# The distance stage of an attention kernel: key part first, by columns, query part second, by rows, stored 16 rows at a time

## What is computed

```python
dist_idx = pos_l - pos_r + M - 1
pos_emb = dist_emb[dist_idx]
rel_q = jnp.einsum('bhld,lrd->bhlr', q, pos_emb)
rel_k = jnp.einsum('bhrd,lrd->bhlr', k, pos_emb)
scores = (scores + rel_q + rel_k) / jnp.sqrt(jnp.asarray(D, scores.dtype))
```

## Time before, and how the profile is read

| | |
|---|---|
| median of 3 runs | 3550.53 us (3544.78 to 3551.01) |
| the profiled execution | 3545.81 us, span 3544.3 us |
| distance stage, first add to next stage's first DMA | 401.23 to 1520.00 us |
| first add of the first tile to first add of the last tile | 1077.2 us for 31 tiles |
| mean granted clock of PE in that stretch | 0.66 of full speed |

### The profile page before, as it was taken

How to read it: one execution, slowest core, us unless ns; L and a number is a source line. 1 busy time by engine, 2 the same in 40 slices (tenths; PEclk the granted TensorE clock), 3 DMA queues, 4 the chain that set the end, 5 groups by cost and what they waited for, 6 DMA issues and landing times. The chain is left out here.

```text
span 3544.3 us, 68683 instructions
## 1 busy us (share of the span) xinstructions
PE 2759.8 (78%) x18124; PEld 1931.5 (54%) x18124; DVE 2474.6 (70%) x6213; ACT 1770.8 (50%) x3509; POOL 703.2 (20%) x715
## 2 busy tenths in 40 slices
PE   4676588787787787748888877888888588888887
PEld 2343577777677777625555544555555344444443
DVE  5665477676777677648888877888888566666664
ACT  2343354444454444348888877888888411111111
POOL 2432000000000000012212211212221223333334
PEclk7888566666666666668999998999999789999999
DMA  3999799989989989799999999999999501111110
GB/s 112 221 224 213 162 311 348 294 337 291 331 302 333 299 333 321 309 261 271 268 272 278 267 257 268 268 272 274 270 272 275 180 32 63 62 62 62 62 62 20
DMA packets 905515, 807.89 MB, mean 228 GB/s; under 512 B 236808, under 2 KB 809536, under 8 KB 870832
## 3 DMA queue, kind: packets, MB, share of 16 engines
q1 hardware_dynamic: 840112, 640.95, 60.5%
q0 software_dynamic: 29440, 98.07, 13.0%
q10 hardware_dynamic: 35840, 67.12, 8.3%
HBM read 465.93 MB, written 340.05 MB: 227 GB/s over the span
## 5 line engine op out<-in xcount | busy, mean ns | idle before, releaser
L1059 ACT ACTIVATE t_e<-t_neg,t_low 128x512 f32<-128x512 f32 x1024 | 739.6, 736 | 232.2 <-DVE t_low L1001 228.9
L676 ACT ACTIVATE d_r<-d_pq 128x1024 f32<-128x1024 f32 x512 | 531.7, 1050 | 608.0 <-PE d_pq L633 604.6
L710 DVE TENSOR_TENSOR d_r<-d_pk,d_r 128x1024 f32<-128x1024 f32 x512 | 616.1, 1223 | 272.9 <-ACT d_r L676 134.0
L1001 DVE CUSTOM_DVE_ANT_0 t_neg<-t_ps,t_r 128x512 f32<-128x512 f32 x1024 | 671.3, 687 | 24.3 <-issue 24.3
L644 PE MATMUL d_pk<-d_win,d_k 96*128 96x128 bf16 x4096 | 513.8, 295 | 216.0 <-DVE d_r L710 181.0
L927 PE MATMUL t_pt<-t_ident,t_e 128*128 128x128 f32 x4096 | 639.4, 279 | 1.4 <-DVE t_eT L1009 0.9
L917 PE MATMUL t_ps<-t_kb,t_qa 96*128 (+1 forms) x1024 | 402.0, 393 | 251.6 <-DVE t_low L1001 202.2
L644 PEld LDWEIGHTS d_pk<-d_win,d_k 96*128 96x128 bf16 x4096 | 445.6, 183 | 248.5 <-DVE d_r L710 213.6
L927 PEld LDWEIGHTS t_pt<-t_ident,t_e 128*128 128x128 f32 x4096 | 513.7, 144 | 110.4 <-ACT t_eT L1066 16.7
L633 PE MATMUL d_pq<-d_win,d_q 96*128 96x128 bf16 x4096 | 498.2, 287 | 62.9 <-DVE d_q L693 45.2
L633 PEld LDWEIGHTS d_pq<-d_win,d_q 96*128 96x128 bf16 x4096 | 442.4, 187 | 80.2 <-DVE d_q L693 45.8
(11 more groups left out here) (134 smaller groups left out, 2509.1 us busy)
## 6 DMA issues: line engine op xcount, KB each, us to landing
r_scratch<-d_r SPq DMA_DIRECT2D x256, 1024.0 KB, 14.2
t_r<-r_scratch SPq DMA_DIRECT2D x1024, 256.0 KB, 5.3
d_q<-q_chunks_scratch ACTq DMA_DIRECT2D x64, 512.0 KB, 10.8
d_q<-q_chunks_scratch ACTq DMA_DIRECT2D x128, 256.0 KB, 14.1
t_kb<-k_chunks_scratch POOLq DMA_DIRECT2D x32, 512.0 KB, 19.9
q_chunks_scratch<-a_part SPq DMA_DIRECT2D x96, 128.0 KB, 3.6
q_rows_scratch<-a_part SPq DMA_DIRECT2D x96, 128.0 KB, 2.2
k_chunks_scratch<-a_part SPq DMA_DIRECT2D x96, 128.0 KB, 3.5
```

Of the source, the lines that this page charges most:

```text
L676: nc.scalar.activation(r[lc % 2][:, n * QL:(n + 1) * QL, :], pq[n % 2][:], ACT.Copy).then_inc(q_out, 1)
L710: nc.vector.tensor_tensor(part, pk[n % 2][:].rearrange("p r l -> p l r"), part, ALU.add).then_inc(k_added, 1)
L1001: nc.vector.tensor_tensor_reduce(out=neg[:, L, :], in0=p_s[bank(j, L)][:], in1=r[:, j % RR, L].rearrange("p c r -> p (c r)"), scale=-0.25, ...
L1059: nc.scalar.activation(e[:, j % 2, L, :], neg[:, L, :], ACT.Exp, bias=low[:, j % 2, L:L + 1], scale=-1.0, accum_out=total[:, j // GH, L, j ...
```

## The change

The two parts change places. ACT now fills a tile with the key part: `fill` waits for a k unit, and copies it into 8 columns of all 128 rows, reading PSUM with the axes exchanged. DVE then adds q unit after q unit, 8 whole rows each. PE does `q_unit(n)` of the tile in hand and `k_unit(n - 4)` of the next. Since rows become final in order, SP issues each store of 16 rows after the two adds that finish it. Since a column touches all rows, ACT waits at unit 0 for all eight stores of the tile two before. The loads and copies of `q` and `k` move with their users.

```diff
@@ PE
-                              k_unit(col, lc, n)
+                              q_unit(col, lc, n)
                           if n >= LEAD and more:
-                              q_unit(col + (lc + 1) // NT, (lc + 1) % NT, n - LEAD)
+                              k_unit(col + (lc + 1) // NT, (lc + 1) % NT, n - LEAD)
@@ ACT
 def load_q(col, lc, u):
+    later(act, q_units, NU * (NT * col + lc - 1) + HU * (u + 1))
...
-    act.wait_ge(q_units, NU * tile + n + 1)
-    later(act, r_stored[lc % 2][n * NP // NU], 16 * (NT // 2 * col + lc // 2))
-    nc.scalar.activation(r[lc % 2][:, n * QL:(n + 1) * QL, :], pq[n % 2][:], ACT.Copy).then_inc(q_out, 1)
-    if n % HU == HU - 1 and more:
-        load_q(col + (lc + 1) // NT, (lc + 1) % NT, n // HU)
+    act.wait_ge(k_units, NU * tile + n + 1)
+    if n == 0:
+        for p in range(NP):
+            later(act, r_stored[lc % 2][p], 16 * (NT // 2 * col + lc // 2))
+    nc.scalar.activation(r[lc % 2][:, :, n * KR:(n + 1) * KR], pk[n % 2][:].rearrange("p r l -> p l r"),
+                         ACT.Copy).then_inc(k_out, 1)
+    if n % HU == HU - 1 - LEAD % HU and not (isinstance(tile, int) and tile == 0):
+        load_q(col, lc, n // HU)
@@ DVE
-    dve.wait_ge(q_out, NU * (tile + 1))
+    dve.wait_ge(k_out, NU * (tile + 1))
     for n in range(NU):
-        dve.wait_ge(k_units, NU * tile + n + 1)
-        part = r[lc % 2][:, :, n * KR:(n + 1) * KR]
-        nc.vector.tensor_tensor(part, pk[n % 2][:].rearrange("p r l -> p l r"), part, ALU.add).then_inc(k_added, 1)
-        if n == 1 and more: copy_q(*nxt, 0)
-        if n == 4 and lc == 0: copy_k(col, 1)
-        if n == 9 and more: copy_q(*nxt, 1)
-        if n == NU - 1 and lc == NT - 1 and not last: copy_k(col + 1, 0)
+        dve.wait_ge(q_units, NU * tile + n + 1)
+        part = r[lc % 2][:, n * QL:(n + 1) * QL, :]
+        nc.vector.tensor_tensor(part, pq[n % 2][:], part, ALU.add).then_inc(q_added, 1)
+        if n == 1 and lc == NT - 1 and not last: copy_k(col + 1, 0)
+        if n == 5: copy_q(col, lc, 1)
+        if n == 9 and lc == NT - 1 and not last: copy_k(col + 1, 1)
+        if n == NU - 1 and more: copy_q(col + (lc + 1) // NT, (lc + 1) % NT, 0)
@@ SP
-    sp.wait_ge(k_added, NU * (g * NT * NT + tile + 1))
     for p in range(NP):
+        sp.wait_ge(q_added, NU * (g * NT * NT + tile) + UP * (p + 1))     # UP = 2 units
         sp.dma_start(to, r[u][:, p * part:(p + 1) * part, :] ...)
```

More of the change, by code:

```diff
@@ L608, in column @@
                         base = nc.gpsimd.snap(base)
-                    for lc in range(NT - 1):
+                    for lc in range(NT - 2):
                         load_win(col, base, lc)
@@ L612, in column @@
                     load_k(col, 1)
-                    load_win(col, base, NT - 1)
+                    for lc in range(NT - 2, NT):
+                        load_win(col, base, lc)
                 column(0)
@@ L639, in k_unit @@
                         pe.wait_ge(k_copied[u], col + 1)
-                    later(pe, k_added, NU * tile + n - 1)
+                    if n == 0:
+                        pe.wait_ge(win_loaded[lc], 16 * (col + 1))
+                    later(pe, k_out, NU * tile + n - 1)
                     for a in range(KR):
@@ L668, in load_q, with fill @@
                                       .rearrange("b r h w -> r b (h w)")).then_inc(q_loaded[u], 16)
[L670 removed]
+                def fill(col, lc):
                     tile = NT * col + lc
                     for n in range(NU):
[L673 to L685 removed]
+                        act.wait_ge(k_units, NU * tile + n + 1)
+                        if n == 0:
+                            for p in range(NP):
[4 more added lines that the diff above has]
+                            load_q(col, lc, n // HU)
+                def column(col, last=False):
+                    for lc in range(1, NT):
+                        fill(col, lc)
+                    if not last:
+                        fill(col + 1, 0)
+                for u in range(2):
+                    load_q(0, 0, u)
+                fill(0, 0)
                 columns(act, column)
@@ L727, in _, with store @@
             def _(sp):
+                def store(g, tile, u):
+                    UP = NU // NP
+                    for p in range(NP):
+                        sp.wait_ge(q_added, NU * (g * NT * NT + tile) + UP * (p + 1))
+                        part = TB // NP
+                        to = r_d[g][tile % NT, tile // NT, :, p * part * TB:(p + 1) * part * TB]
+                        sp.dma_start(to, r[u][:, p * part:(p + 1) * part, :].rearrange("n l r -> n (l r)")
+                                     ).then_inc(r_stored[u][p], 16)
                 for g in range(ng):
@@ L730, in _ @@
                         for u in range(2):
-                            tile = 2 * pair + u
-                            sp.wait_ge(k_added, NU * (g * NT * NT + tile + 1))
[L734 to L738, removed]
+                            store(g, 2 * pair + u, u)
                 for u in range(2):
```

33 lines of the change are left out of this document (14 added, 19 removed).

## The result

The changed kernel takes 3505.5 us in the median of four runs (3500.4 to 3507.0), the kernel before 3547.7: ratio 0.988, 95% interval 0.986 to 0.990. The forecast was 3510 us, with a range of 3455 to 3565. (The 3547.7 is of four runs of the kernel before; the 3550.5 ahead of the prediction was of the first three.) The profiled execution takes 3506.3 us where the one before took 3545.8, so 39.5 us less, and the stage accounts for it: from the first add to the next stage's first DMA it takes 1118.8 us before and 1074.3 after, 44.5 less, and its first add comes 5.4 later.

The account below looks back on a forecast made before the run. PE's pace, stalls by copies and the boundary were taken as the path. Tiles -27 us, the stage's end -14.5 and start +1 gave -40 from 3545.8, so 3505; plus 4.7 for the runs' median, 3510 us, range 3455 to 3565.

Parts of the forecast that it names:

- order of adds and copies: DVE's sequence within a tile, worked out: unit 15 ends at 25.84 us instead of 27.8, a gain of 2.0.
- Plain tile: A tile that is not a column's last: 31.6 us instead of 33.6, so -2.0 us in each of 24.
- the boundary: DVE's idle time between two tiles: 5.2 us, growing by 1.8 to 7.0 through ACT's three issues of q.
- Last tile of a column: Tile with both key copies among its adds: 31.6 + 3.0 for copies + 2.0 for late keys, 36.6 us.
- PE's pace, plus the stalls by copies, plus the boundary: Path claimed to set a tile of the kernel before: 33.0 us, 33.9 with the DMA wait.
- the 0.9 of DMA wait may go too: DVE's wait for q's second half in a tile: 0.9 us that might vanish besides the 2.0 gained.
- Free, by 6 us: ACT's new wait at unit 0 for all eight stores: 12 us of room, 6 allowed for the last store.
- R3: Slower rival: the store wait takes over, ACT's unit 0 comes 2.3 us late per tile, 3581 us; chance 0.11.
- ACT's hop: ACT's fill reading PSUM with a hop on every element: taken as 1050 ns, bounds 1050 and twice that.
- The clock: PE's faster pace, 1.43 instead of 1.71 us, for four units of a plain tile: 1.1 us gained.
- R1: Rival: PE's clock stays fast from unit 4 on, 30.1 us a tile, store work of 30.6 binds, 3461 us; chance 0.13.
- The ends: Stage's end: 27.1 us for 41.6, -14.5, with only the last stores left; stage's start: +1 us (0 to 4).

Follow-up runs that it names:

- e4: Changed kernel with q loaded for the first two tiles only, copies and waits kept: 3424.7 us, ratio 0.964 to the kernel before.
- e9: Changed kernel with q's second half issued by POOL, ahead of the keys' second half in POOL's queue: 3447.2 us, ratio 0.973 to the kernel before.
- e3: Changed kernel with the keys loaded for the first column only, copies and waits kept: 3454.2 us, ratio 0.973 to the kernel before.
- e12: Changed kernel with the keys' second half issued by ACT, in q's queue behind q's second half: 3475.1 us, ratio 0.979 to the kernel before.
- e2: Kernel before, with DVE's copy of q's first half moved behind a tile's last add, two tiles ahead: 3536.9 us, ratio 0.996.
- e6: Kernel before, with q loaded for the first two tiles only and the copy of q's first half moved behind the last add: 3444.2 us, ratio 0.968.
- e1: Changed kernel, but SP waits for all 16 adds of a tile before issuing its eight stores: 3877.1 us, ratio 1.092 to the kernel before.
- e7: Changed kernel with q's loads issued by SP in the stores' queue, between stores: 3601.5 us, ratio 1.013 to the kernel before.

## Why the prediction was right, point by point

The forecast lay 4.5 us beside the result, and that closeness is luck: two of its terms were wrong by some 30 us each, in opposite directions. What was right by reasoning is the order of adds and copies, the fill's time, the clock's part of a plain tile, and the end of the stage.

- **Plain tile.** Forecast -2.0 us each, -48 over 24; measured -3.3, -79. The hand-made order of adds and copies was exact. The step that failed is the boundary: sized 7.0, it is 5.5 in the median. Without issues in it, it is 4.9 (e4, e9), so ACT's issues cost 0.6 there instead of 1.8, and the 5.2 read from one tile stood for 4.9.
- **Last tile of a column.** Forecast +3.0, +21 over seven; measured +7.1, +50. The copies cost the 3.0 that they were priced at (e3); the wait, sized at 2 us and put on the keys at unit 1, came out as 7.4: 4 to 8 us on q at unit 5, with a wait for a store beside it in four of the seven. The forecast was 31.6 + 3.0 + 2.0, measured are 30.3 + 3.0 + 7.4. This is the largest mis-sized term. The prediction had the work of such a tile at hand, 28.5 + 9 us of DMA, and did not hold it against its own 36.6. But work alone would not have given it either: with the same work in another queue the tile takes 36.3 (e12).
- **"PE's pace, plus the stalls by copies, plus the boundary" as the path of the kernel before.** This step failed in its reason. The sum fitted (33.0, with the DMA wait 33.9), but the wait for q absorbs what is taken from the rest: e2 gained 0.4 us a tile where 2.0 stood in the prediction. The place of the copy is worth 2.2 us only where q is in time (e6). In the changed kernel it is in time, and not because the stores no longer go out in a burst: e1 has the burst, and q lands as soon. What e1 and the changed kernel share is the issue 4.3 us earlier against the tile's end, ahead of the burst, with a landing after some 12 us for 19. So -2.0 for the copy and "the 0.9 of DMA wait may go too" are one effect, and it comes with the issues among the last fills, which the prediction booked as a cost alone. No run issued q earlier in the kernel before, so that half is argued.
- **The stores.** "Free, by 6 us" held in plain tiles, but by some 3 us: the last store lands 8.6 us after its issue in the median, where 6 were allowed and the room is 11. It did not hold in four of the seven last tiles, so the sign named for R3, a wait of ACT for a store, did come, in them alone. e1 shows what the new wait costs without the early issue (11.4 us a tile), e7 with 1 MB ahead of the last store.
- **ACT's hop.** Right, 1030 ns. The ratio in the Trainium skill's page "Vector Engine (DVE) Microarchitecture Reference", section "Measured stream behaviour on trn2", 1.73 to 1.054, would have made an estimated 1.7 us of 1050 ns (the prediction says 1.6); the trace disagrees for PSUM on this engine as well. What the rows show for DVE is 1223 ns for 1024 elements, 1.19 each; the split into 1.04 and 0.15 is shown by none of them.
- **The clock.** R1 did not happen: the mean of the stage is 0.66, before and after. The term of -1.1 in a plain tile was right: from first to last add it takes 24.7 us in the mean, 1.2 less than the 25.84 worked out at the lower level, and in the tile shown the last adds come at the faster pace. (R1's 30.6 us "of store work" are all of a mean tile's DMA work; the stores are 20 of it.)
- **The ends.** -14.5, as forecast. The start was +5.4 for +1 (0 to 4), outside its own bounds: the first half of the keys landed at 385.6, ten microseconds after the first half of q had in the kernel before, where 2 stood in the prediction.

Sum of what was measured: 24 x (-3.3) + 7 x 7.1 = -29.5, -14.5, +5.4: -38.6 of the 39.5.

## What to carry to other kernels

A wait that is small and regular can be the thing that sets a loop: before pricing a shorter path, ask when the late load would land if everything else were faster. When an exchange of loops makes a buffer final bit by bit, it also makes it wanted whole at once; the early stores and the late wait must be sized together, and a load in the queue ahead of the last store cost 88 us here (e7). Two loads with different deadlines did better in one queue, in the order of their deadlines, than in two (e12, e9). And the place of an issue is a term with two sides: three issues among the last fills cost 0.6 us a tile, and brought the load ahead of the burst of stores.

## What the hardware did that I had not expected

Reading PSUM with a hop of 512 bytes between elements costs nothing on ACT (1030 ns for 1024 elements a partition, 1050 in order) nor on DVE (1223 and 1223). A DMA share of 1.00 over a whole tile did not mean that the DMA engines set its length: 30.3 us at 1.00, 29.5 at 1.02 with the same bytes (e9), and 29.1 at 0.71 with a fifth of the bytes gone (e4). A load of 1 MB took 12 us to land when it was issued just ahead of a burst of eight stores of 1 MB (e1) and 19 when issued 3.6 us behind its start (the kernel before). A turn of the loop cost PE 2.8 us in e4 and 6 to 8 in all other runs, so it is no constant of the kernel. And the same 1 MB of keys, issued at the same moment, cost 4.4 us a tile more in a queue of its own than behind the load that was needed first (e12).
